# A gated cross-attention and FFN block: the scores of a unit pair moved behind the values of another, with new engine orders

## What is computed

```python
# x, ctx: (32, 64, 512) f32 -> 2048 rows, 8 chunks of 256 rows
Q = layernorm(x) @ Wq.T      # 32 heads of 128, in 8 groups of 4
K = ctx @ Wk.T; V = ctx @ Wv.T   # 8 heads of 128
S = Q K.T * 128**-0.5, causal inside each batch of 64 rows
x = x + tanh(g_xattn) * (softmax(S) V) @ Wd.T
a, b = layernorm(x) @ Wgate.T, layernorm(x) @ Wup.T   # 1792 wide, W = w * (su @ sv)
x = x + tanh(g_ffn) * (silu(a) * b) @ Wdown.T
```

## Time and profile before

| | us |
|---|---|
| median of three runs | 1430.93 |
| profiled execution | 1430.72 |
| its span, first to last instruction | 1428.7 |
| PE busy | 1400.6 (98%) |
| DVE busy | 1016.2 (71%) |
| POOL busy | 1038.6 (73%) |
| ACT busy | 640.3 (45%) |

### The profile page before, as it was taken

How to read it: one execution, slowest core, us unless ns; L and a number is a source line. 1 busy time by engine, 2 the same in 40 slices (tenths; PEclk the granted TensorE clock), 3 DMA queues, 4 the chain that set the end, 5 groups by cost and what they waited for, 6 DMA issues and landing times.

```text
span 1428.7 us, 19944 instructions
## 1 busy us (share of the span) xinstructions
PE 1400.6 (98%) x6810; PEld 1125.3 (79%) x6810; DVE 1016.2 (71%) x1549; ACT 640.3 (45%) x1246; POOL 1038.6 (73%) x919
## 2 busy tenths in 40 slices
PE   8999999999999999999999999999999999999998
PEld 8988788888887767777776766767888888888887
DVE  6487777777465677777776776775688878676776
ACT  6465555554444344443443444444344434343433
POOL 5599999998879556656656777775678886666664
PEclk9999999999999999999999999999999999999999
DMA  8477787778887745434443433331112112212112
GB/s 282 150 251 226 233 270 257 253 254 282 307 264 264 254 156 199 140 125 142 135 152 118 155 116 120 127 132 31 45 45 60 52 45 65 105 47 65 45 59 74
DMA packets 116067, 217.96 MB, mean 153 GB/s; under 512 B 9472, under 2 KB 47616, under 8 KB 113920
## 3 DMA queue, kind: packets, MB, share of 16 engines
q1 hardware_dynamic: 115968, 216.70, 46.1%
HBM read 151.13 MB, written 65.54 MB: 152 GB/s over the span
## 4 chain that ended last, share of the span: by engine, by line
PE 82%; POOL 8%; DVE 4%; issue 3%; ACT 1%; DMA 1%; SPq 0%; DVEq 0%; POOLq 0%; ACTq 0%
PE bank L574 65%; PE bank L848 3%; PE bank L849 3%; PE bank L850 3%; PE bank L697 3%; PE bank L722 3%; POOL prob L1663 2%; POOL xn L1677 1%; POOL wd_lo L1649 1%; POOL prob L1657 1%; POOL prob L1669 1%; DVE X L1386 1%; POOL wa_lo L1643 1%; PE bank L621 1%; DMA q_sb<-q_scratch 0%
## 5 line engine op out<-in xcount | busy, mean ns | idle before, releaser
L574 PE MATMUL bank<-xc,wa_hi 128*128 128x512 f32 x896 | 277.4, 391 | 0.0
L574 PE MATMUL bank<-wd_hi,o_hi 128*128 128x512 f32 x512 | 207.9, 406 | 5.0 <-issue 3.5
L574 PE MATMUL bank<-wd_lo,o_hi 128*128 128x512 f32 x512 | 200.8, 392 | 0.0
L574 PE MATMUL bank<-wd_hi,o_lo 128*128 128x512 f32 x512 | 199.5, 390 | 0.0
L574 PEld LDWEIGHTS bank<-xc,wa_hi 128*128 128x128 f32 x896 | 167.7, 188 | 36.4 <-issue 1.1
L574 PE MATMUL bank<-xc,wa_lo 128*128 128x512 f32 x448 | 174.5, 390 | 0.0
L1455 DVE SCALAR_TENSOR_TENSOR X<-bank,tg,X 128x512 f32<-128x512 f32 x221 | 154.5, 742 | 0.0
L574 PE MATMUL bank<-x_hi,wf_hi 128*128 128x512 f32 x392 | 153.0, 390 | 0.0
L574 PE MATMUL bank<-x_hi,wf_lo 128*128 128x512 f32 x392 | 152.6, 389 | 0.0
L574 PE MATMUL bank<-x_lo,wf_hi 128*128 128x512 f32 x364 | 141.7, 389 | 0.0
L1669 POOL TENSOR_TENSOR prob<-prob,row_inv 128x512 f32<-128x512 f32 x64 | 72.5, 1153 | 94.6 <-DVE row_inv L1356 94.6
(11 more groups left out here) (181 smaller groups left out, 3424.7 us busy)
## 6 DMA issues: line engine op xcount, KB each, us to landing
q_scratch<-q_st SPq DMA_DIRECT2D x32, 1024.0 KB, 4.4
q_sb<-q_scratch SPq DMA_DIRECT2D x64, 512.0 KB, 4.9
w_raw<-in_wq SPq DMA_DIRECT2D x32, 512.0 KB, 4.4
wd_raw<-in_wd SPq DMA_DIRECT2D x16, 1024.0 KB, 5.1
f_raw<-ffn_eff_scratch SPq DMA_DIRECT2D x28, 512.0 KB, 3.6
er_raw<-in_sf_r SPq DMA_DIRECT2D x42, 256.0 KB, 3.9
e_raw<-in_wf SPq DMA_DIRECT2D x42, 256.0 KB, 5.4
ffn_eff_scratch<-e_eff SPq DMA_DIRECT2D x42, 256.0 KB, 5.2
```

Source lines behind the costliest of these rows:

```text
L574: last = pe.matmul(to, a, b, start=(start and n == 0), stop=(stop and n == 3 * len(pairs) - 1), skip_group_check=onto)
```

## The change

On PE, `scores(u + 2)` and `scores(u + 3)` stand directly behind the values of a pair and ahead of two outputs; before, the scores stood at the head of a period between two outputs, and the values between two others. Bank 6, which one output in four shares with the scores, therefore serves the outputs with i % 4 == 1 instead of i % 4 == 3, and the waits follow: a pair's scores wait for `add_to_x` of the output made four matmul groups earlier.

```diff
     def output_bank(i):
         if i >= 2 * NU - 4:
             return 4 + i - (2 * NU - 4)
-        return 6 if i % 4 == 3 else (3 * (i // 4) + i % 4) % 2
+        return 6 if i % 4 == 1 or i == 2 * NU - 5 else (3 * (i // 4) + SHARED[i % 4]) % 2
...
             if u >= 6 and u % 2 == 0:
-                pe.wait_ge(v_y, 2 * u - 8)
+                pe.wait_ge(v_y, 2 * u - 10)
...
+        output(0)
         weighted_values(1)
-        output(0)
+        scores(4)
+        scores(5)
         for p in range(2, NPAIR):
             u = 2 * p
-            scores(u)
-            scores(u + 1)
             output(2 * u - 7)
             if p in COLUMNS1:
                 pe.wait_ge(v_o, 2 * u - 4)
...
             weighted_values(u - 1)
+            if p + 1 < NPAIR:
+                scores(u + 2)
+                scores(u + 3)
             output(2 * u - 5)
             output(2 * u - 4)
```

ACT, DVE and POOL get new orders in each period:

```diff
 # ACT
         for p in range(2, NPAIR):
             u = 2 * p
+            exponentials(u)
+            exponentials(u + 1)
+            other_sums(p)
             if p in WD_STEP:
...
                 x2_columns(COLUMNS1[p], (2, 3))
-            other_maxima(p)
             out_hi(u - 2)
-            exponentials(u)
-            exponentials(u + 1)
+            out_hi(u - 1)
             if p in SPLIT1:
                 x2_hi_of(SPLIT1[p])
-            other_sums(p)
+            if p + 1 < NPAIR:
+                other_maxima(p + 1)
             if p == F_FIRST:
                 for part in range(3):
                     gate_up_hi(0, part)
-            out_hi(u - 1)
 # DVE
             add_to_x(2 * u - 8)
-            out_lo(u - 3)
...
             sums(u)
             sums(u + 1)
-            add_to_x(2 * u - 5)
+            add_to_x(2 * u - 7)
             inverse(p)
-            if p in SPLIT1:
-                x2_lo_of(SPLIT1[p])
             if p in ROWS1:
                 stats2(ROWS1[p])
                 ln_moments(8 + ROWS1[p])
+            if p in SPLIT1:
+                x2_lo_of(SPLIT1[p])
+            add_to_x(2 * u - 6)
+            out_lo(u - 2)
+            if p + 1 < NPAIR:
+                turned(u + 2)
+                turned(u + 3)
+            out_lo(u - 1)
+            probs_turned(u)
+            probs_turned(u + 1)
+            add_to_x(2 * u - 5)
+            if p + 1 < NPAIR:
+                maxima(u + 2)
+                maxima(u + 3)
+                row_maxima(p + 1)
 # POOL
-            over_sum(u - 2)
-            over_sum(u - 1)
-            masked(u)
-            masked(u + 1)
-            if p in COLUMNS1:
-                x2_sums(COLUMNS1[p])
+            over_sum(u)
+            over_sum(u + 1)
             if p in WD_STEP:
...
-            less_max(u)
-            less_max(u + 1)
             if p in ROWS1:
                 ln_pow(8 + ROWS1[p])
                 apply2(ROWS1[p])
+            if p + 1 < NPAIR:
+                masked(u + 2)
+                masked(u + 3)
+                less_max(u + 2)
+                less_max(u + 3)
+            if p in COLUMNS1:
+                x2_sums(COLUMNS1[p])
```

More of the change, by code:

```diff
@@ L290, in flamingo @@
     NPAIR = NU // 2
+    SHARED = (0, None, 1, 2)
     def output_bank(i):
@@ L294, in output_bank @@
             return 4 + i - (2 * NU - 4)
-        return 6 if i % 4 == 3 else (3 * (i // 4) + i % 4) % 2
+        return 6 if i % 4 == 1 or i == 2 * NU - 5 else (3 * (i // 4) + SHARED[i % 4]) % 2
     def output_before(i):
-        n = 3 * (i // 4) + i % 4 - 2
-        return 4 * (n // 3) + n % 3
+        n = 3 * (i // 4) + SHARED[i % 4] - 2
+        return 4 * (n // 3) + SHARED.index(n % 3)
     def score_bank(u):
@@ L500, in _ @@
                 load_v(3)
+                load_q_k(6)
+                load_q_k(7)
             if q == Q0 + NHP:
@@ L532, in _ @@
             u = 2 * p
-            for n in range(u + 2, min(u + 4, NU)):
-                load_q_k(n)
             load_v(u)
             load_v(u + 1)
+            for n in range(u + 4, min(u + 6, NU)):
+                load_q_k(n)
             if p == 4:
@@ L735, in output @@
                 pe.wait_ge(a_c11, NQ)
-            elif i == 1:
+            elif i == 2:
                 pe.wait_ge(v_t2, NQ)
-            elif i < 2 * NU - 4 and i % 4 == 3:
-                pe.wait_ge(v_turn, min(2 * ((i + 5) // 4), NU - 2) + 1)
+            elif i < 2 * NU - 4 and i % 4 == 1:
+                pe.wait_ge(v_turn, min((i + 7) // 2, NU - 2) + 1)
+            elif i == 2 * NU - 5:
+                pe.wait_ge(v_y, i - 1)
             elif i < 2 * NU - 4:
@@ L1181, in _ @@
         other_maxima(1)
+        out_hi(1)
         exponentials(2)
@@ L1184, in _ @@
         other_sums(1)
-        out_hi(1)
+        other_maxima(2)
         for p in range(2, NPAIR):
             u = 2 * p
+            exponentials(u)
+            exponentials(u + 1)
+            other_sums(p)
             if p in WD_STEP:
@@ L1300, in quad @@
             v.tensor_tensor(t2[:, :], bank[1][:, :], s1[:, :], ALU.add).then_inc(v_t2, 1)
+            if q == NQ - 1:
+                maxima(2)
+                maxima(3)
+                v.wait_ge(a_tanh, 1)
+                out_lo(0)
             if q >= NQ - 2:
@@ L1479, in _ @@
             quad(q)
[L1480 to L1483, removed]
         row_maxima(1)
+        out_lo(1)
         sums(2)
         sums(3)
+        turned(4)
+        turned(5)
         inverse(1)
+        probs_turned(2)
+        probs_turned(3)
+        maxima(4)
+        maxima(5)
+        row_maxima(2)
         for p in range(2, NPAIR):
@@ L1510, in _ @@
                 ln_moments(8 + ROWS1[p])
+            if p in SPLIT1:
[13 more added lines that the diff above has]
+                row_maxima(p + 1)
         add_to_x(2 * NU - 8)
-        out_lo(NU - 3)
-        probs_turned(NU - 2)
-        probs_turned(NU - 1)
         for i in range(2 * NU - 7, 2 * NU - 4):
@@ L1787, in _ @@
         less_max(3)
+        over_sum(2)
+        over_sum(3)
+        masked(4)
+        masked(5)
+        less_max(4)
+        less_max(5)
         for p in range(2, NPAIR):
             u = 2 * p
-            over_sum(u - 2)
-            over_sum(u - 1)
-            masked(u)
-            masked(u + 1)
-            if p in COLUMNS1:
-                x2_sums(COLUMNS1[p])
+            over_sum(u)
+            over_sum(u + 1)
             if p in WD_STEP:
@@ L1808, in _ @@
                     ffn_left_lo(0, part)
-        over_sum(NU - 2)
-        over_sum(NU - 1)
         for n in range(NF):
```

## The result

The changed kernel takes **1508.58 us** (median of 4 runs, 1507.84 to 1508.70) against 1431.88 (4 runs, 1430.73 to 1434.05) of the kernel before in the same comparison: a ratio of 1.0533, with a 95% interval of 1.0514 to 1.0551. The forecast was about 1505, 3.6 us less.

The account below looks back on a forecast made before the run. PE alone bounded attention before; the new orders were to make it wait on a loop over DVE, POOL and ACT. 5.9 + 54 + 6 + 9 = 75 us on 1430.7 gave about 1505 us, 8-in-10 range 1470 to 1524.

Parts of the forecast that it names:

- the four long waits: PE in attention: scores for X, values for xb (about 6.7 us), outputs for o_lo (about 7), exit for wd_lo (7.5).
- Ordinary periods: Sixteen periods, p = 2 to 18: the loop over add_to_x takes 15.54 us against PE's 15.17, +5.9 us.
- ROWS1 and COLUMNS1: FFN side work in p = 18 on: late masks and ACT's copies behind the softmax hold values u + 1, 7.3 us over 15.54.
- four are 255: Rounds, p = 18 to 30: each 63.8 us, so four are 255 against 201.1 before, +54 us.
- SPLIT1: Side work period: x2_lo on DVE waits for ACT's x2_hi, delaying both out_lo; next scores 7.1 us late.
- The clock: Behind long PE gaps the clock falls to 1.2 GHz; charged 1.6 us, in SPLIT1 1.15.
- the rival in which the clock stays up: No clock falls behind the gaps: rounds lose 11 us less, entry and exit 3, giving 1491 us; chance 0.15.
- Entry: Start of attention: pair 2's softmax comes late, scores 6 4.4 us later, plus one clock fall of 1.6; +6 us.
- Exit: p = 30: output 120 waits 7.5 us for the last wd_lo, plus one clock fall of 1.6; +9 us.
- side waits was hidden: Rival: the wait in SPLIT1 or COLUMNS1 ends with something that came anyway, 33 us less, 1472 us; chance 0.12.
- More contention: Rival: POOL's passes stretched by DVE's long subtraction, a second clock fall per gap, 12 us and more, 1520; chance 0.10.
- PE stays the bound, faster: Rival: one switch between kinds of matmul saved per period, waiting in the rounds gone too, 1410 us; chance 0.04.

Follow-up runs that it names:

- swap_wd: Changed kernel with wd_lo ahead of over_sum on POOL; 1505.37 us.
- cols_early: Changed kernel with x2_columns first in its period on ACT, ahead of the exponentials; 1489.85 us.
- apply_split: Changed kernel with apply2's second tile behind the masks on POOL in ROWS1 periods; 1498.01 us.
- lo_late: Changed kernel with x2_lo_of behind row_maxima of its period on DVE, instead of ahead of both out_lo; 1490.33 us.
- entry_new: Changed kernel with another entry order on ACT and DVE, starting pair 2's softmax ahead of out_hi(1) and the turned scores; 1505.05 us.
- exit_later: Changed kernel with the split of the first FFN weights one period later on ACT and POOL; 1505.57 us.
- all_eight: Changed kernel with seven mended orders on ACT, DVE and POOL, plus out_lo(u - 1) back ahead of the turned probabilities in ROWS1 periods only; 1419.32 us.

## Why the prediction was right, step by step

**What bounds and how it was followed: right.** The method, one period followed from semaphore to semaphore with durations of the trace of before, gave the loop within 0.04 us (15.54 forecast, 15.58 and 15.56 found) and named the four long waits.

**Ordinary periods, +5.9: 9.4 found, the step that was mis-sized.** Of the stretch's 11.0 us, 1.6 are the clock behind the entry (17.22 us to the next scores instead of 15.58), which the prediction counts in the entry. The rest is 9.4. The failing line is "the two `wd_lo` end at 5.45" in the list of inputs that "come in time": output 2u - 4 was put at 4.75 a few words on, so by its own numbers `wd_lo` came 0.7 late. Found: a wait of 0.75. `swap_wd` takes it away and gives 3.0 of the 3.5 us that the term was short of; the rest is the loop's 15.58 in place of 15.54. PE's own period, taken at 15.17 "or somewhat less", was 14.91. The disturbed periods are 15.92, so 1.01 over that. The 0.26 that the wait of 0.75 leaves over are in how a wait is listed: a bracket counts from the listed end of an output's matmul, 0.39 us behind its start, while the next one starts 0.23 behind it where nothing is waited for; and the first matmul behind the wait is followed after 0.31. Of the 1.01, 0.67 lie in the slack that PE has against the loop of 15.58, and 0.34 count.

**ROWS1 and COLUMNS1, 6.7 us of wait: 6.39 in the first round, then 5.01, 5.46 and 4.88.** The mechanism stands (cols_early, apply_split). The step that failed is the one from one round to four, "four are 255", each like the first: something is carried over, from SPLIT1 into the next round. The SPLIT1 periods ahead of rounds two to four took 24.35, 23.90 and 24.48 us, so 1.7, 1.25 and 1.8 more than the 22.65 at which the prediction has DVE ready, and the xb waits end 1.4, 1.0 and 1.55 us earlier than in the first round. When the stall is taken away (lo_late) they are long again.

**The 51.8 against 54 is in part luck.** The three periods of a round were put at 22.87, 17.14 and 23.79 us. Over four rounds the first ones took 2.3 us less than that and the second ones 1.6 less, and the third ones, SPLIT1, 1.6 more, since a fall of the clock costs more there than the 1.6 charged.

**SPLIT1, about 7 us: 6.78, four times.** ACT and DVE of the changed kernel in the first of these periods:

```profile
821.86 1.70 ACT L1077 ACTIVATE x_hi<-xb 128x1792 fp32r<-128x1792 f32 x1
...
823.59 2.02 DVE L1426 TENSOR_TENSOR x_lo<-xb,x_hi 128x1792 fp32r<-128x1792 f32 x1 [6.58 <-ACT x_hi L1077]
```

`x2_lo` starts 7.7 us behind the scores at 815.89 (7.8 forecast), DVE had been idle for 6.58 us for it, and both `out_lo` follow. Shown by lo_late.

**The clock.** It fell behind each of attention's ten waits of over 4 us, as the 3.48 and 3.37 us of scores that take 1.95 show, and behind the wait at the exit the window says how far:

```profile
1054.00:1058.00 4.00, 3.87 (x9) 3.11 (x10) 0.66 (x2) 0.00 (x0) 0.00 (x0) 0.51 0.60 197
```

The third column from the right is the granted clock: 0.51, the 1.2 GHz level. The Trainium skill, TensorE: Matmul & The Clock Gate, Part 1, has idleness take the engine to that level; for these ten waits the trace agrees, and the rival in which the clock stays up falls. One premise of that rival was misread, though. It says that in the other three rounds before, gaps of one to two us passed without a fall; one of the three was as long as the gap at 834 that was followed by one:

```profile
935.54 1.95 PE L697 MATMUL bank<-q_sb,k_sb 128*64 128x256 f32 x16 [2.76 <-DVE X L1386]
```

The granted clock was 1.00 behind it. So the kernel before shows gaps of 2.75 us going either way, and the prediction was right to charge its longer ones, but "2.75 us of idleness sufficed" is half of what the rows say. What a fall costs is not one number either. Behind the xb waits eight values come first, which took 2.01 us in the first three rounds and 1.91 in the fourth, instead of 1.07, and then the scores, 3.48, 2.53, 3.68 and 2.74: with both, 2.5, 1.5, 2.7 and 1.6 us were lost. Behind the o_lo waits outputs start 0.43 us apart instead of 0.23, for 8 to 11 matmuls, which is 1.9 to 2.5 us each time. At the entry and the exit it is 1.6 and 1.8. The prediction's 1.6 is at the lower side of what was lost; it had left out the values, and the outputs in SPLIT1.

**Entry, 4.4 + 1.6: 4.9 + 1.6. Exit, 7.5 + 1.6: a wait of 7.79 at 1054.13, 9.6 in all.** Both right, and entry_new and swap_wd move them as they should. That the exit's wait comes from the split standing ahead of the last pair's exponentials is shown by the `wd_lo` wait's going in exit_later; the 9 us could not be had there, since another wait took its place.

**The rivals.** None of the side waits was hidden. More contention is not seen either, rather less. `over_sum` by line on the pages, of before and of after:

```profile
L1669 POOL TENSOR_TENSOR prob<-prob,row_inv 128x512 f32<-128x512 f32 x64 | 72.5, 1153 | 94.6 <-DVE row_inv L1356 94.6
```

```profile
L1688 POOL TENSOR_TENSOR prob<-prob,row_inv 128x512 f32<-128x512 f32 x64 | 65.8, 1049 | 92.9 <-DVE row_inv L1372 92.9
```

Before, it fell on `x2_lo` once a round, and the pair took 3.71 us instead of 2.06 each time, which is 6.6 of the 6.7 us between the two rows; in the new order POOL is idle while DVE makes `x2_lo`. "PE stays the bound, faster" had the switch at 0.2 us a period and it is 0.26, and its point of decision, 0.4 us a period, was well chosen: one `out_lo` moved on DVE is enough to pass it. What it asked of the rounds was too much for this change, but not for the layout.

Not tried: `all_eight`'s side work orders with the scores at their old place. So what the new place adds over the old one, with both as well ordered, is known for ordinary periods alone (0.26 us each).

## What to carry to other kernels

When instructions are laid out anew around a loop, follow every input of the engine that bounds, each against the time at which it is wanted, with the slack of the new period and not of the old one; an input that is late by half a microsecond counts once per period. Ask of each piece of occasional side work what stands behind it in its queue: here a copy, a subtraction and two passes of 2 us, moved behind or ahead of the softmax, made most of the 52 us that the rounds lost. And repair waits together, since a stall gives the other engines a lead and hides part of the next one: single edits tell the causes, but not always their prices.

## What was unexpected of the hardware

- A wait's releaser in the trace is a guess where two inputs come close together: o_hi was named for eight waits that ended with `wd_lo`, and moving `wd_lo` on POOL took all eight away.
- The switch between 128x512 outputs and the small matmuls of scores and values costs PE: the first output matmul behind those is followed after 0.34 us and the last ahead of them after 0.31, against 0.23 in between. With the same matmuls and one such stretch of small ones per period instead of two, the period is 14.91 instead of 15.17 us, 0.26 less.
- A longer wait is not always followed by a dearer fall of the clock: in the changed kernel waits of 5.01, 5.46 and 6.39 us lost 1.5, 2.7 and 2.5 us behind them. And shorter waits go either way: one of 2.76 us (before) and one of 2.59 (entry_new) were followed by scores at their 1.95 us, one of 2.61 (`all_eight`) by 2.74, and one of only 2.16 (cols_early, at 855.81) by 3.54.
